# Top-2 experts of layers 0 and 3: an inverse map from one-hot products, gathers and scatters tile by tile, no halves

## The reference, cut to what matters

```python
# layer 0, called twice: x = x + ffn(layernorm(x))
probs = softmax(x @ router_w.T);  vals, idx = top_k(probs, 2)
for e in range(8):
    w = sum(where(idx == e, vals, 0), axis=-1)
    out = out + w[:, None] * (gelu(x @ w1[e].T) @ w2[e].T)
# layer 3, called twice
val, idx = top_k(x @ router_w.T + router_b, 2);  weights = softmax(val)
h1, h2 = split(x @ wa[e].T + ba[e], 2);  y = (silu(h1) * h2) @ wb[e].T + bb[e]
```

## Time and profile before

| | us |
|---|---|
| median of 3 executions (5238.81 to 5245.73) | 5244.28 |
| profiled execution, its own time | 5242.22 |
| its span | 5240.4 |
| layer 0, first expert step | 248.3 to 543.3 |
| layer 0, second expert step | 728.9 to 1031.0 |
| layer 3, first expert step | 4193.4 to 4580.5 |
| layer 3, second expert step | 4843.7 to 5231.3 |

### The profile page before, as it was taken

How to read it: one execution, slowest core, us unless ns; L and a number is a source line. 1 busy time by engine, 2 the same in 40 slices (tenths; PEclk the granted TensorE clock), 3 DMA queues, 4 the chain that set the end, 5 groups by cost and what they waited for, 6 DMA issues and landing times. The chain is left out here.

```text
span 5240.4 us, 72223 instructions
## 1 busy us (share of the span) xinstructions
PE 3619.5 (69%) x21562; PEld 2395.2 (46%) x21562; DVE 3436.4 (66%) x6736; ACT 2318.3 (44%) x4211; POOL 1742.7 (33%) x1640
## 2 busy tenths in 40 slices
PE   5757557588873568882577777479936959577594
PEld 4657347533322423332422322246634649555494
DVE  4522661379996368864389999678857647665485
ACT  3335324355541347770444444347734525343252
POOL 0043104456661435551334445102211132300323
PEclk9968768799996779995778888679966869788697
DMA  2022002212210232310311111000000012100122
GB/s 98 2 62 79 11 5 83 81 59 65 65 64 14 82 92 87 89 29 19 120 45 51 51 49 58 9 19 1 1 3 3 0 36 68 51 4 2 34 68 61
DMA packets 263213, 238.46 MB, mean 46 GB/s; under 512 B 32569, under 2 KB 216992, under 8 KB 262032
## 3 DMA queue, kind: packets, MB, share of 16 engines
q1 hardware_dynamic: 242448, 193.00, 12.4%
q0 software_dynamic: 20480, 41.98, 2.7%
HBM read 159.03 MB, written 74.97 MB: 45 GB/s over the span
## 5 line engine op out<-in xcount | busy, mean ns | idle before, releaser
L2030 DVE TENSOR_TENSOR_SCAN s_l_attn_a_h<-s_l_attn_a_da,XN 128x512 f32<-128x512 f32 x512 | 598.3, 1210 | 55.7 <-issue 35.1
L646 POOL DMA_INDIRECT slots_x<-XN,s_l_ffn_ffn_slots x320 | 310.1, 969 | 797.6 <-DVE s_l_ffn_ffn_slots L525 556.3
L1972 PE MATMUL s_l_attn_a_y_ps<-XN,c_ident 128*128 128x512 f32 x1024 | 545.1, 657 | 35.5 <-DVE s_l_attn_a_y L2302 28.9
L1980 ACT ACTIVATE s_l_attn_a_da<-s_l_attn_a_delta,s_l_attn_a_a 128x510 f32<-128x510 f32 x512 | 345.1, 685 | 466.8 <-DVE s_l_attn_a_h L2030 463.3
L654 POOL DMA_INDIRECT s_l_ffn_ffn_back<-slots_y,s_l_ffn_ffn_slots x320 | 305.7, 955 | 515.3 <-DMA slots_y<-PICK 289.6
L550 DVE COPY s_l_ffn_ffn_xt<-s_l_ffn_ffn_turned 128x128 f32<-128x128 f32 x416 | 120.2, 290 | 537.3 <-PE s_l_ffn_ffn_turned L706 535.0
L481 ACT COPY s_l_ffn_ffn_own_w<-up 128x512 f32 (+2 forms) x416 | 304.9, 734 | 300.1 <-DVE s_l_ffn_ffn_expert_no L534 193.0
L1990 POOL TENSOR_TENSOR XN<-s_l_attn_a_h,LOG 128x512 f32<-128x512 f32 x256 | 319.8, 1272 | 305.2 <-DVE s_l_attn_a_h L2030 285.1
L717 PE MATMUL s_l_ffn_ffn_up<-s_l_ffn_ffn_xt,s_l_ffn_ffn_own_w 128*128 128x128 f32 x2944 | 413.0, 282 | 7.0 <-DVE s_l_ffn_ffn_shifted_a L558 5.6
L725 PE MATMUL s_l_ffn_ffn_down<-down,s_l_ffn_ffn_hid 128*128 x2944 | 407.8, 279 | 12.9 <-DVE s_l_ffn_ffn_hid L563 6.3
L1990 POOL TENSOR_TENSOR XN<-s_l_attn_a_h,s_l_attn_a_more_c_rows 128x512 f32<-128x512 f32 x256 | 321.0, 1275 | 243.6 <-DVE s_l_attn_a_h L2030 165.1
(11 more groups left out here) (651 smaller groups left out, 8115.6 us busy)
## 6 DMA issues: line engine op xcount, KB each, us to landing
LOG<-s_l_attn_a_c_kept SPq DMA_DIRECT2D x128, 256.0 KB, 3.0
s_l_attn_a_more_c_rows<-s_l_attn_a_c_kept SPq DMA_DIRECT2D x128, 256.0 KB, 3.1
XNT<-slots_x SPq DMA_DIRECT2D x64, 320.0 KB, 5.3
slots_y<-LOG SPq DMA_DIRECT2D x16, 640.0 KB, 4.3
slots_y<-PICK SPq DMA_DIRECT2D x16, 640.0 KB, 4.3
s_l_attn_b_qr<-s_l_attn_b_q_rows SPq DMA_DIRECT2D x64, 144.0 KB
s_l_attn_b_kr<-s_l_attn_b_k_rows SPq DMA_DIRECT2D x64, 144.0 KB
XNT<-slots_x SPq DMA_DIRECT2D x16, 384.0 KB, 4.5
```

The source lines that it names most:

```text
L646: nc.gpsimd.indirect_dma_start(k.slots_x[h][0:NH * P, :], bass.IndirectOffsetOnAxis(slots[:, c, t:t + 1], 0), k.XN[:, t, :], None).then_in ...
L1972: last = self.nc.tensor.matmul(self.y_ps[:, i, :], self.k.ident[:], self.hc[n % 2][:, i, :], start=(n == 0 and not begun), stop=(n == NST ...
L1980: self.nc.scalar.activation(self.da_half(g, n, i)[:, :, 1:], self.delta[par][:, i, :].rearrange("p (b t) -> p b t", b=BPG)[:, :, 1:], ACT. ...
L2030: self.nc.vector.tensor_tensor_scan(self.h[n % 2][:, i, :], self.da_half(g, n, i).rearrange("p b t -> p (b t)"), self.u[n % 2][:, i, :], 0 ...
```

## The change

`sorted_experts` takes the place of `sparse_experts` for layers 0 and 3. All 4096 tokens are sorted at once into 71 tiles (64 and 7). `layer_norm` also stores `XN` in token order (`rows_x`) by two plain DMAs. Instead of scattering rows to slots, the kernel works out the inverse: which pair stands in each slot. For each of the 64 columns of pairs, DVE compares slot starts with the 71 tile starts (`in_tile`) and slot places with the 128 lanes (`in_place`), ACT scales the first by the pair's number, and PE adds up 64 products of 71 columns into one table `inverse`. From it come the row that each lane fetches (`from_row`) and the row to which its result goes (`to_row`).

Then POOL gathers each tile directly from `rows_x` and scatters each result directly to `rows_y`, which is in token order, the two choices side by side; a ring of 8 tiles each way, and scatters run 5 (layer 0) or 6 (layer 3) tiles behind gathers. When all scatters have landed, SP fetches `rows_y` in 8 pieces of 4 tiles, and DVE adds them to `X`. The bias of layer 3 is kept in `XN` and added during the first tiles. The zero fill at the start covers 48 tiles of `slots_x` and 128 rows of `rows_x`; each step loads 9 constants, not 5.

```diff
+            sp.dma_start(k.rows_x[TOKENS:TOKENS + P, :], flat(k.PICK[:])[:, 0:D]).then_inc(k.rows_stored, 16)
             for h in range(2):
-                for first in range(0, 40, fill_tiles):
+                for first in range(0, 24, fill_tiles):
...
+            if store_rows:
+                rows = k.rows_x[0:TOKENS, :].rearrange("(p t) d -> p t d", t=TILES)
+                for h in range(2):
+                    sp.wait_ge(rows_ready, (h + 1) * GROUPS // 2)
+                    half = slice(h * TILES // 2, (h + 1) * TILES // 2)
+                    sp.dma_start(rows[:, half, :], k.XN[:, half, :]).then_inc(k.rows_stored, 16)
...
+def sorted_experts(nc, k, name, consts, up_chunks, chunks, gated=False):
+    NT = 2 * TILES + 7
+    PAIRS, SPAN = 2 * TILES, 8
+    RING, LAG = 8, 6 if gated else 5
+    PIECE = 4
...
+            for g in range(PAIRS // SPAN):
+                if g >= 4:
+                    dve.wait_ge(placed, g - 3)
+                nc.vector.tensor_tensor(in_tile[g % 4], per_pair(start[:], g, NT), per_span(tile_start[:], NT), ALU.is_equal).then_inc(hot, 1)
+                nc.vector.tensor_tensor(in_place[g % 4], per_pair(place[:], g, P), per_span(lane[:], P), ALU.is_equal).then_inc(hot, 1)
...
+            dve.wait_ge(placed, PAIRS // SPAN)
+            nc.vector.scalar_tensor_tensor(out=pad[:], in0=inverse, scalar=0.0, in1=spare[:], op0=ALU.is_equal, op1=ALU.mult)
+            dve.drain()
+            nc.vector.scalar_tensor_tensor(out=row[:], in0=inverse, scalar=-1.0, in1=pad[:], op0=ALU.add, op1=ALU.add)
+            dve.drain()
+            nc.vector.tensor_scalar(from_row[:], row[:], spare_lane[:, 0:1], None, ALU.min)
+            dve.drain()
+            nc.vector.tensor_scalar(from_row[:], from_row[:], 1, None, ALU.logical_shift_right).then_inc(rows_known, 1)
+            nc.vector.tensor_copy(to_row[:], row[:]).then_inc(rows_known, 1)
...
+            def add_bias(g):
+                dve.wait_ge(bias_kept, g + 1)
+                some = k.X[:, g * GT:(g + 1) * GT, :]
+                nc.vector.tensor_tensor(some, some, k.XN[:, g * GT:(g + 1) * GT, :], ALU.add)
+            def combine(i):
+                dve.wait_ge(returned[i], 16)
+                h, first = divmod(i * PIECE, TILES // 2)
+                for c in range(2):
+                    for t in range(PIECE):
+                        at = i * PIECE + t
+                        nc.vector.scalar_tensor_tensor(out=k.X[:, at, :], in0=both[h][:, first + t, c, :], scalar=gates[:, c, at:at + 1], in1=k.X[:, at, :],
+                                                       op0=ALU.mult, op1=ALU.add)
+                    dve.drain()
+                for t in range(i * PIECE, (i + 1) * PIECE):
+                    nc.vector.bn_stats(k.stats[:, t, :], k.X[:, t, :])
...
+            def scale(g):
+                act.wait_ge(hot, 2 * g + 1)
+                for n in range(SPAN):
+                    last = nc.scalar.activation(in_tile[g % 4][:, n, :], in_tile[g % 4][:, n, :], ACT.Copy, scale=row_no[:, g * SPAN + n:g * SPAN + n + 1])
+                last.then_inc(scaled, 1)
+            def keep_bias(g):
+                act.wait_ge(bias_up, g + 1)
+                nc.scalar.copy(k.XN[:, g * GT:(g + 1) * GT, :], bias_ps[g % 4]).then_inc(bias_kept, 1)
...
+            def gather(j):
+                since(pool, turned_up, j - RING + 1)
+                nc.gpsimd.indirect_dma_start(xin[j % RING], None, k.rows_x[:, :],
+                                             bass.IndirectOffsetOnAxis(from_row[:, j:j + 1], 0)).then_inc(gathered[j % RING], 16)
+            def scatter(j):
+                pool.wait_ge(y_ready, j + 1)
+                nc.gpsimd.indirect_dma_start(k.rows_y[:, :], bass.IndirectOffsetOnAxis(to_row[:, j:j + 1], 0),
+                                             yout[j % RING], None).then_inc(scattered[j % RING], 16)
...
+            pool.wait_ge(k.rows_stored, 16 * k.stores)
+            pool.wait_ge(rows_known, 1)
+            for j in range(NT):
+                gather(j)
+                if j == LAG:
+                    pool.wait_ge(rows_known, 2)
+                if j >= LAG:
+                    scatter(j - LAG)
+            for j in range(NT - LAG, NT):
+                scatter(j)
+        @block.sync
+        def _(sp):
+            for i in range(RING):
+                sp.wait_ge(scattered[i], 16 * (moved[i] + len(range(i, NT, RING))))
+            for i in range(TILES // PIECE):
+                h, first = divmod(i * PIECE, TILES // 2)
+                src = k.rows_y[0:2 * TOKENS, :].rearrange("(p t c) d -> p t c d", t=TILES, c=2)
+                sp.dma_start(both[h][:, first:first + PIECE, :, :], src[:, i * PIECE:(i + 1) * PIECE, :, :]).then_inc(returned[i], 16)
...
+                for g in range(EARLY):
+                    add_up(g)
+            for g in range(PAIRS // SPAN):
+                pe.wait_ge(hot, 2 * g + 2)
+                pe.wait_ge(scaled, g + 1)
+                for n in range(SPAN):
+                    pair = g * SPAN + n
+                    last = nc.tensor.matmul(inverse, in_place[g % 4][:, n, :], in_tile[g % 4][:, n, :], start=(pair == 0), stop=(pair == PAIRS - 1))
+                last.then_inc(placed, 1)
+            if gated:
+                for g in range(EARLY, GROUPS):
+                    add_up(g)
+                pe.wait_ge(bias_kept, GROUPS)
+            pe.wait_ge(experts_ready, 1)
...
-        consts, loads = sparse_consts(nc, k, s)
-        layer_norm(nc, k, name + "_ln", k.bufs["L0_ffn_router"], 8, loads=loads)
+        consts, loads = sorted_consts(nc, k, s)
+        layer_norm(nc, k, name + "_ln", k.bufs["L0_ffn_router"], 8, loads=loads, store_rows=True)
         softmax8(nc, k, name + "_gate", False)
-        sparse_experts(nc, k, name + "_ffn", consts, 2, 4, 4)
+        sorted_experts(nc, k, name + "_ffn", consts, 4, 4)
```

More of the change, by code:

```diff
@@ L187, in take_stats, with layer_norm @@
         nc.vector.bn_stats(flat(k.stats[:, bass.ds(first + t, 1), :]), tile(k.X, first + t))
-def layer_norm(nc, k, name, project=None, n_out=0, loads=()):
+def layer_norm(nc, k, name, project=None, n_out=0, loads=(), store_rows=False):
     with Scope(nc, name) as s:
         stats, stats_taken = k.stats, k.stats_taken
+        if store_rows:
+            k.stores += 2
         k.stats_taken = False
@@ new lines, in sorted_consts @@
+def sorted_consts(nc, k, s):
+    landed = s.sem("consts_landed")
+    shapes = [("c_before", [P, P]), ("c_not_first_tile", [P, 8 * TILES]), ("c_steps32", [P, TILES]), ("c_tile_no71", [P, 71]),
+              ("c_row_no", [P, 2 * TILES]), ("c_lane", [P, P]), ("c_tile_start", [P, 71]), ("c_spare_row", [P, 71]), ("c_spare_lane", [P, 1])]
+    bufs = {n: s.sb(n, shape) for n, shape in shapes}
+    bufs["landed"], bufs["loads"] = landed, 16 * len(shapes)
+    return bufs, [(bufs[n][:], k.dram[n], landed) for n, _ in shapes]
@@ L750, in l0_ffn @@
     with Scope(nc, name) as s:
[L751 to L752 removed]
+        consts, loads = sorted_consts(nc, k, s)
+        layer_norm(nc, k, name + "_ln", k.bufs["L0_ffn_router"], 8, loads=loads, store_rows=True)
         softmax8(nc, k, name + "_gate", False)
[L754 removed]
+        sorted_experts(nc, k, name + "_ffn", consts, 4, 4)
 def l3_ffn(nc, k, name):
     with Scope(nc, name) as s:
[L759 to L760 removed]
+        consts, loads = sorted_consts(nc, k, s)
+        layer_norm(nc, k, name + "_ln", k.bufs["L3_ffn_router"], 8, loads=loads, store_rows=True)
         softmax8(nc, k, name + "_gate", True, k.bufs["L3_ffn_rb"])
[L762 removed]
+        sorted_experts(nc, k, name + "_ffn", consts, 8, 4, gated=True)
 def claim_by_capacity(nc, k, name):
@@ L3834, in layouts @@
     o["c_tile_no"] = np.broadcast_to(np.arange(40, dtype=np.float32), (P, 40))
+    o["c_steps32"] = np.broadcast_to(P * np.arange(TILES, dtype=np.float32), (P, TILES))
+    o["c_tile_no71"] = np.broadcast_to(np.arange(71, dtype=np.float32), (P, 71))
+    o["c_tile_start"] = P * o["c_tile_no71"]
+    o["c_lane"] = np.broadcast_to(-np.arange(P, dtype=np.float32), (P, P))
+    own = TILES * np.arange(P, dtype=np.float32)[:, None] + np.arange(TILES, dtype=np.float32)
+    o["c_row_no"] = np.concatenate([2 * own + c + 1 for c in range(2)], axis=1)
+    o["c_spare_lane"] = 2 * TOKENS + 2 * np.arange(P, dtype=np.float32)[:, None]
+    o["c_spare_row"] = o["c_spare_lane"] + 2 * P * o["c_tile_no71"] + 1
     o["c_early_first"] = np.broadcast_to(np.repeat(8 - np.arange(8, dtype=np.float32), TILES), (P, 8 * TILES))
@@ L3961, in build @@
         k.down = k.keep("down", [P, max(dram[f"L{i}_ffn_w2"].shape[1] for i in (0, 1, 3))])
-        k.slots_x, k.slots_y = ([nc.dram_tensor(f"slots_{x}{h}", (40 * P, D), F32, kind="Internal").ap() for h in range(2)] for x in "xy")
+        k.slots_x, k.slots_y = ([nc.dram_tensor(f"slots_{x}{h}", (24 * P, D), F32, kind="Internal").ap() for h in range(2)] for x in "xy")
+        k.rows_x = nc.dram_tensor("rows_x", (TOKENS + P, D), F32, kind="Internal").ap()
```

(4 more changed lines are left out.)

236 lines of the change are left out of this document (added).

## The result

| | before | after |
|---|---|---|
| median of the executions, us | 5241.55 (4, 5233.61 to 5245.73) | 5126.62 (4, 5120.34 to 5130.06) |
| ratio, 95% interval | | 0.9781 (0.9764 to 0.9798) |
| profiled execution's span | 5240.4 | 5125.5 |

A forecast was written before the change was run, and what follows sets the result against it. Layer 0's tiles were PE-bound, with half of POOL's DMAs uncovered before and behind them and DVE's adds after; layer 3 alike. Zero fill -5, layer 0 -22 and layer 3 -125 make -152 from 5242.2: 5090, median 5092, range 5050 to 5165.

The forecast's parts named there:

- POOL the bound of layer 0's tiles: Layer 0's tiles: POOL's two indirect DMAs take 2.52 us a tile where PE needs 1.93, so POOL bounds them.
- the earlier start: Start of each expert step: first transpose at 320 instead of 336.5 in layer 0, 4272 instead of 4288.6 in layer 3.
- The inverse table: Before the first gather of each step: eight groups last 15 to 29 us by PE's clock; 22 taken, 20 in layer 3.
- Three bias products now come before the inverse and warm PE: Layer 3, start of the step: they warm PE, so the inverse was taken as 20 us.
- the table is slow: Rival, inverse table in four steps: PE's clock low throughout, DVE's compares dearer, 30 to 35 us; +10 a step, 5132; 14%.
- POOL's 136 DMAs: Layer 0 after the first kept result: 71 scatters and 65 gathers at 1.26 us each, 171 us, from 327 to 498.
- The tail: After layer 0's last scatter lands: 3.5 us for SP's first piece, 25.5 of DVE adds; 20 us shorter than before.
- the meeting of the engines: Between a step's last DVE work and the next step's start: 3.1 us, the middle, where 5.8 stood.
- Layer 3: Each of two steps: first transpose at 4272, 71 tiles at 2.97 us, end at 4518.6 instead of 4581.0; -62 a step.
- the rival at 5280: Rival, layer 0's tiles: PE's clock stays at 1.2 GHz, 3.86 us a tile, +95 a step; 3% (9% for a third low, 5155).
- The stretched DMAs: Rival: every indirect DMA takes 1.55 us, 5190, 5%, or 1.67, 5255, 1%; layer 3's tiles alone stretched, 5115, 8%.
- The zero fill: Kernel's head: fewer zero-fill DMAs by SP, so what waits behind them starts earlier; -5 us, or 0 if the weights' load hides it.

The follow-up runs named there:

- the run with plain fetches: Against the changed kernel, SP fetches layer 3's tiles by plain DMAs of neighbouring (wrong) rows, POOL only scatters; 5120.6 us, ratio 0.9771.

## Why the prediction was right, and what was mis-sized

**Right.** The mechanism held at each place: POOL the bound of layer 0's tiles, PE of layer 3's, the earlier start, the tail of 26 us of adds, and most of the gain in layer 3. 5126.6 lies in the range of 5050 to 5165, just above the main case's own 5055 to 5125 and 35 us above the 5092. One part did not come at all: layer 0 was to give 11 us a step and gave nothing. The total stays in the range all the same because 125 of the 152 us forecast were layer 3's, which gave 117.

**The inverse table** is the term that was off most. "So the eight groups last 15 us if PE keeps up, 29 if its clock stays low ... I take 22, the middle"; it was the low end of the clock, 27.55 and 27.26 us. The earlier trace rows held both ends, and also the row that decides: 8-column products left a low clock low, and I set against it a bias product of 512 columns that raised it. The first transpose of layer 0 came 44.5 us after the mask's copy, not 38 (+6.4), that of layer 3 46.2 instead of 38 (+8). "Three bias products now come before the inverse and warm PE" failed as a step of its own. They did raise the clock, but only in their last half microsecond; then PE waited 2.73 us for the first group, and in that group the clock was back at 0.50. Only with two more products and 1.02 us of wait did it hold. Four times 6 to 8 is 29 of the 37 us missing. The nearest rival was "the table is slow", 5132, given 14%; it wanted 30 to 35 us.

**The first tiles of layer 0.** From first transpose to first scatter were 8.8 us, where the forecast had 7 (320 to 327): +1.8.

**POOL's 136 DMAs.** 181.7 us, where 171.4 were forecast: +10.3. 3.4 are the price, 0.97 and 1.00 us with 0.30, so 1.285 and not 1.26; 7.2 are waits of scatters (15.6 less the first, 4.2, and 14 issues of 0.30). "The lag of 5 tiles is 12.6 us; ... 10, so the scatter's wait is just covered" held for most tiles and failed in this step for every fifth or sixth, whose gather PE awaited 1.4 to 2 us. In the second step hardly a gather was late: 176.4 us, +5.0.

**The tail.** The first piece came 0.8 us sooner than forecast, the adds took 26.05 us against 25.5, and "I take 3.1, the middle" for the meeting of the engines was 0.36 in the first step of either layer, in place of 5.83: -2.7. Behind layer 0's second step it was 2.52 in place of 7.57, with POOL's last DMA as far back, so that DMA is not all that holds the meeting; no run tests it. These terms make 15.6 for layer 0's first step, and -11 + 15.6 = +4.6 stands for the +4.8 measured.

**Layer 3.** 8.2 for the table, -0.4 for landing and adds, 0.4 for the tiles, -2.7 for the meeting: +5.5 on -62, and -57.3 was measured. That the tiles hit 211 with 211.4 is luck in part: the steady pace was 2.82 and not 2.97, and some late gathers and the first and last tiles took the difference.

**The clock in layer 0's tiles** stayed at 1.00 with PE busy 81%; the rival at 5280 did not come. **The stretched DMAs**: scatters of layer 3 took some 1.17 us on the timeline and those of layer 0 0.99, most gathers 0.96 in both. Two DMAs with 0.30 each are then 2.73, under PE's 2.82, which is why the run with plain fetches gained only 4 us a step there. The prediction had no row for which DVE instruction does it; the changed kernel's timeline has. In the line before each of these scatters DVE multiplies two buffers of SBUF, and the second scatter lies beside that product for longer:

```profile
4399.67 0.69 DVE L898 TENSOR_TENSOR s_l_ffn_ffn_hid<-s_l_ffn_ffn_silu,s_l_ffn_ffn_shifted_b 128x512 f32<-128x512 f32 x1
4400.07 1.17 POOL L1000 DMA_INDIRECT rows_y<-PICK,s_l_ffn_ffn_to_row  x1 [0.38 <-ACT PICK L955]
4401.54 0.96 POOL L995 DMA_INDIRECT XNT<-rows_x,s_l_ffn_ffn_from_row  x1 [0.30 <-issue]
...
4408.38 0.68 DVE L898 TENSOR_TENSOR s_l_ffn_ffn_hid<-s_l_ffn_ffn_silu,s_l_ffn_ffn_shifted_b 128x512 f32<-128x512 f32 x1
4408.53 1.41 POOL L1000 DMA_INDIRECT rows_y<-PICK,s_l_ffn_ffn_to_row  x1 [0.38 <-ACT PICK L955]
```

From 4300 to 4490 the 12 scatters that lie beside such an instruction for less than 0.1 us take 1.00 on average, the 30 with 0.1 to 0.3 us take 1.16, the 18 with 0.3 to 0.5 take 1.22. Gathers do the same: 53 with less than 0.3 us take 0.96, the 11 with more take 1.2 on average, one 1.43. The product keeps its 0.69 us. The Trainium skill, page SBUF — State Buffer, section Who interferes with whom, has a VectorE instruction with two SBUF inputs contend with a GpSimd instruction that reads SBUF, and not with one that only writes it; the prediction left that condition out. These DMAs have their row lists in SBUF, layer 3 has such a product a tile and layer 0 none, so the trace agrees as far as the DMA's side goes; it does not show the product held up. By the rule as by the row nothing moved in the sum.

**The zero fill** gave 2.9 and not 5: PE's first transposes came 7 us earlier, and the attention block behind them took back four.
